# A fused transformer block on one core: three value products ahead of the loop's branch, spare weights kept in DRAM, rope products left in PSUM

## The reference, cut to what matters

```python
qkv = x @ w_qkv.T                       # 3 * 512 columns, 16 heads of 32
q, k = rope(q), rope(k)                 # pairs (even, odd) turned by cos and sin of the position
scores = q @ k.T * 32 ** -0.5           # only keys at most 63 rows back
attn = softmax(scores) @ v
x = layernorm(x + attn @ w_out.T)
gate = silu((x @ w_gate) * s_gate)      # int8 weights, 512 x 2048
up = (x @ w_up) * s_up
x = layernorm(x + ((gate * up) @ w_down) * s_down)
```

## Time and profile before

| | us |
|---|---|
| median of 3 runs | 1215.11 (1214.43 to 1217.15) |
| the profiled execution | 1210.73 |
| its span (first to last instruction) | 1208.9 |
| TensorE busy | 1159.1 (96%) |
| VectorE busy | 977.0 (81%) |
| ScalarE busy | 641.1 (53%) |
| GpSimd busy | 645.0 (53%) |
| mean granted TensorE clock, share of full | 0.991 |

### The profile page before, as it was taken

How to read it: one execution, slowest core, us unless ns; L and a number is a source line. 1 busy time by engine, 2 the same in 40 slices (tenths; PEclk the granted TensorE clock), 3 DMA queues, 4 the chain that set the end, 5 groups by cost and what they waited for, 6 DMA issues and landing times.

```text
span 1208.9 us, 25954 instructions
## 1 busy us (share of the span) xinstructions
PE 1159.1 (96%) x8601; PEld 606.4 (50%) x8601; DVE 977.0 (81%) x2727; ACT 641.1 (53%) x1777; POOL 645.0 (53%) x605
## 2 busy tenths in 40 slices
PE   9997999989999899998999989999899999999998
PEld 4444546445464454645446454464545546455444
DVE  7898988878887789877998779987699879986434
ACT  3954785038851479405794059922588127871330
POOL 0787675336753467525585166742577336752330
PEclk9999999999999999999999999999999999999999
DMA  9995895458844597534966269660795507944200
GB/s 289 181 183 120 152 201 127 105 85 158 138 105 109 81 171 136 130 76 72 193 116 148 57 94 197 115 144 36 124 180 110 136 36 142 194 85 105 87 1 35
DMA packets 360555, 149.78 MB, mean 124 GB/s; under 512 B 310096, under 2 KB 332752, under 8 KB 360400
## 3 DMA queue, kind: packets, MB, share of 16 engines
q1 hardware_dynamic: 334976, 106.86, 49.9%
q0 software_dynamic: 19008, 31.98, 9.3%
q10 hardware_dynamic: 6416, 9.00, 2.0%
HBM read 39.53 MB, written 8.39 MB: 40 GB/s over the span
## 4 chain that ended last, share of the span: by engine, by line
PE 55%; issue 16%; POOL 11%; DVE 8%; DMA 6%; ACT 3%; SPq 1%; POOLq 0%; DVEq 0%; ACTq 0%
PE bank L876 34%; PE bank L1148 18%; POOL fuse L768 7%; DMA y<-xT_sb 4%; POOL xT_sb L656 2%; PE bank L1083 2%; ACT bank L1384 1%; DVE fuse L1538 1%; POOL fuse L661 1%; DVE qkT L1601 1%; PE bank L1063 1%; DMA out<-x 1%; DMA xT_sb<-xT 1%; ACT fuse L1285 1%; PE bank L902 1%
## 5 line engine op out<-in xcount | busy, mean ns | idle before, releaser
L876 PE MATMUL bank<-x1T,wg 128*128 128x512 f16 (+1 forms) x1032 | 242.5, 378 | 1.2 <-DVE wg L1644 1.2
L876 PE MATMUL bank<-x1T,wu 128*128 128x512 f16 x1024 | 241.9, 379 | 0.0
L1384 ACT ACTIVATE bank<-bank,neg_max,qk_scale 128x128 f32<-128x128 f32 x512 | 220.3, 434 | 31.5 <-DVE neg_max L1693 30.3
L1148 PE MATMUL bank<-wd,fuse 128*128 128x512 f16 (+2 forms) x1056 | 222.7, 373 | 0.0
L661 POOL TENSOR_TENSOR fuse<-ffn_tmp,fuse 128x512 f16<-128x512 f32 x128 | 148.4, 1159 | 96.1 <-ACT fuse L1285 95.8
L768 POOL TENSOR_TENSOR fuse<-fuse 128x512 f16<-128x512 f32 x116 | 147.4, 1304 | 91.4 <-ACT fuse L1285 88.3
L656 POOL TENSOR_TENSOR xT_sb<-probs,xT_sb 128x512 f16<-128x512 f32 x112 | 129.9, 1160 | 79.4 <-ACT xT_sb L1285 79.2
L1148 PEld LDWEIGHTS bank<-wd,fuse 128*128 128x128 f16 x1056 | 101.9, 98 | 117.9
L876 PEld LDWEIGHTS bank<-x1T,wu 128*128 128x128 f16 x1024 | 100.2, 98 | 120.6
L876 PEld LDWEIGHTS bank<-x1T,wg 128*128 128x128 f16 x1032 | 96.4, 98 | 112.1 <-DVE wg L1644 1.4
L1295 ACT ACTIVATE ffn_tmp<-bank,tanh_scale 128x512 f32<-128x512 f32 x128 | 88.5, 692 | 72.1 <-PE bank L876 46.5
(11 more groups left out here) (238 smaller groups left out, 1903.4 us busy)
## 6 DMA issues: line engine op xcount, KB each, us to landing
wg<-w_gate POOLq DMA_DIRECT2D x16, 1024.0 KB, 5.3
wu<-w_up POOLq DMA_DIRECT2D x9, 1024.0 KB, 8.4
v_cross<-v_own SPq DMA_DIRECT2D x64, 128.0 KB, 3.1
out<-x ACTq DMA_DIRECT2D x31, 256.0 KB, 2.0
xT_sb<-xT SPq DMA_DIRECT2D x30, 256.0 KB, 3.8
qkT<-x SPq DMA_DIRECT2D x28, 256.0 KB, 3.4
wu<-w_up POOLq DMA_DIRECT2D x7, 512.0 KB, 5.8
wqkv<-w_qkvT SPq DMA_DIRECT2D x8, 256.0 KB, 6.5
```

The costliest lines, as they stand in the source:

```text
L876: last = pe.matmul(dst, lhsT, rhs, start=(i == 0 and not onto), stop=(i == len(pairs) - 1), skip_group_check=onto)
L1148: last = pe.matmul(dst[:, cols], fuse[:, s, z, rows], wd[:, s, cols], start=(s == 0 and z == 0), stop=(s == STEPS - 1 and z == 1))
L1384: last = act.activation(unit, unit, ACT.Exp, bias=neg_max[:, s % 2, h // 3, h % 3:h % 3 + 1], scale=qk_scale[:, 2:3], accum_out=row_sum[:, ...
```

## The change

- TensorE: `values_first(a, 0)`, `values_fifth(a, 0)` and `values_first(a, 1)` stand at the end of the pass before (`begin_values`), ahead of the branch. `values_first` waits for `rope_done` where it waited for `rope_read`.
- The three sums of the value weights are made once, in `first()`, stored to DRAM by GpSimd, and loaded each tile by ScalarE (768 KB) after the last `up`.
- The late columns are cast once to float16 in DRAM, in `first()`, and loaded from there by ScalarE behind `gate_tanh(f, 2)`, 1 MB and 768 KB (row 3 of `wu` is no longer overwritten); GpSimd's casting loads at step 2 are gone.
- ScalarE's order at the head of a pass: `split_high(2)` stands behind `keep_values_sixth(a, 1)`, and `keep_values_seventh(a, 1)` ahead of `split_high(3)`, where it stood behind `keep_v(a, 1)`.
- Rope: two of four products of a block are written back into their own bank, and the sums read one operand there.
- VectorE, end of attention: `keep_o(7)` and three `add_back_o` stand ahead of three of the four row sums of pair 0.

```diff
@@ gpsimd
+            def keep_v_weights():
+                pool.wait_ge(v_weights_added, 2)
+                pool.sem_inc(passed, 1)
+                pool.wait_ge(v_weights_in[0], 16)
+                pool.dma_start(kept_v_weights, wu[:, 0:KC - 1, LATE:].bitcast(F32)).then_inc(v_weights_kept, 16)
-            def reload_late_columns(a, f, attn):
-                wait(*((v_low, pool, a, NB - 1) if attn else (proj_read, pool, f, NB - 1)))
-                pool.sem_inc(passed, 1)
-                for src, dst in ((w_gate, wg), (w_up, wu)):
-                    done(late_columns_in, pool.dma_start(dst[:, :, LATE:],
-                                                         src.rearrange("(k p) n -> p k n", p=P)[:, :, LATE:]), 16)
...
+                pool.dma_start(wu[:, KC - 1:, LATE:], w_up.rearrange("(k p) n -> p k n", p=P)[:, KC - 1:, LATE:])\
+                    .then_inc(wffn_in, 16)
+                for src, kept, rows in ((w_gate, late_gate, slice(0, KC)), (w_up, late_up, slice(0, KC - 1))):
+                    pool.dma_start(kept, src.rearrange("(k p) n -> p k n", p=P)[:, rows, LATE:]).then_inc(late_kept, 16)
                 sum_w(3)
...
-                if more:
-                    add_v_weights(a + 1, f)
@@ tensor
             def values_first(a, i):
-                wait(rope_read, pe, a, i)
+                wait(rope_done, pe, a, i)
             def values_fifth(a, i):
                 wait(x_summed, pe, a - 1, 7)
-                wait(v_weights_added, pe, a - 1, 2)
+                wait(v_weights_in, pe, a - 1, 15)
-            def project_values(a):
+            def begin_values(a):
                 values_first(a, 0)
                 values_fifth(a, 0)
                 values_first(a, 1)
+
+            def project_values(a):
                 values_sixth(a, 0)
...
                 if more:
                     for i in range(2):
                         project_pair(a + 1, i)
+                    begin_values(a + 1)
@@ scalar
+            def reload_late_columns(a, f, attn):
+                wait(*((v_low, act, a, NB - 1) if attn else (proj_read, act, f, NB - 1)))
+                act.sem_inc(passed, 1)
+                act.wait_ge(v_weights_kept, 16)
+                act.sem_inc(passed, 1)
+                act.wait_ge(late_kept, 2 * 16)
+                for kept, dst in ((late_gate, wg[:, :, LATE:]), (late_up, wu[:, 0:KC - 1, LATE:])):
+                    done(late_columns_in, act.dma_start(dst, kept), 16)
+
+            def load_v_weights(f):
+                wait(up_done, act, f, STEPS - 1)
+                done(v_weights_in, act.dma_start(wu[:, 0:KC - 1, LATE:].bitcast(F32), kept_v_weights), 16)
...
                     keep_values_sixth(a, 0)
-                    split_high(a, 2, ffn)
                     keep_values_fifth(a, 1)
                     keep_values_seventh(a, 0)
                     keep_values_sixth(a, 1)
+                    split_high(a, 2, ffn)
+                    keep_values_seventh(a, 1)
                     split_high(a, 3, ffn)
                     keep_v(a, 0, ffn)
                     keep_v(a, 1, ffn)
-                    keep_values_seventh(a, 1)
...
                     gate_tanh(f, s)
+                    if s == 2:
+                        reload_late_columns(a, f, attn)
...
                 keep_fuse_high(f, STEPS - 1)
+                if more:
+                    load_v_weights(f)
@@ vector
-                    i = (0, 3, 1, 2)[part]
+                    i = ((3, 0, 1, 2) if ffn else (0, 3, 1, 2))[part]
                     src = (even, odd, odd, even)[i]
+                    dst = src if ffn and part % 2 else place[i]
...
-                dve.tensor_tensor(place[0], place[0], place[1], ALU.subtract)
-                done(rope_done, dve.tensor_tensor(place[2], place[2], place[3], ALU.add))
+                dve.tensor_tensor(place[0], even, place[1], ALU.subtract)
+                done(rope_done, dve.tensor_tensor(place[2], odd, place[3], ALU.add))
...
                     add_outer_kept(a, 0)
+                    keep_o(a, STEPS // 2 - 1)
+                    add_back_o(a, 1)
+                    add_back_o(a, 2)
+                    add_back_o(a, 3)
                     add_inner_kept(a, 0)
                     add_inner(a, 0)
                     add_outer(a, 0)
                     proj_added(a, 0)
-                    keep_o(a, STEPS // 2 - 1)
-                    add_back_o(a, 1)
-                    add_back_o(a, 2)
-                    add_back_o(a, 3)
```

More of the change, by code:

```diff
@@ L177, in build @@
         LAST_BANKS = (6, 7)
+        late_gate = nc.dram_tensor("late_gate", (P, KC, INTER // 2), F16, kind="Internal").ap()
+        late_up = nc.dram_tensor("late_up", (P, KC - 1, INTER // 2), F16, kind="Internal").ap()
+        kept_v_weights = nc.dram_tensor("kept_v_weights", (P, KC - 1, INTER // 4), F32, kind="Internal").ap()
         def ev(name, per_tile):
@@ L214, in build @@
         v_added = ev("v_added", NB)
-        v_weights_added = ev("v_weights_added", 3)
+        v_weights_added = sem("v_weights_added")
+        v_weights_kept = sem("v_weights_kept")
+        v_weights_in = ev("v_weights_in", 16)
         v_weights_lessened = sem("v_weights_lessened")
+        late_kept = sem("late_kept")
         o_product = ev("o_product", 12)
@@ L691, in lessen_v_weights, with add_v_weights @@
                 pool.tensor_tensor(low_right, low_right, low_left, ALU.subtract).then_inc(v_weights_lessened, 1)
-            def add_v_weights(a, f):
+            def add_v_weights():
                 low_left, right_less_left, high_left, high_right = v_quarters()
                 second, third, fourth = (added_v_weights(n) for n in range(3))
-                if isinstance(a, int) and a == 1:
-                    pool.wait_ge(v_weights_lessened, 1)
-                else:
-                    wait(up_done, pool, f, STEPS - 1)
-                done(v_weights_added, pool.tensor_tensor(second, high_right, right_less_left, ALU.subtract))
-                wait(v_weights_added, pool, a - 1, 0)
-                done(v_weights_added, pool.tensor_tensor(fourth, high_left, second, ALU.subtract))
-                done(v_weights_added, pool.tensor_tensor(third, second, low_left, ALU.subtract))
+                pool.wait_ge(v_weights_lessened, 1)
+                pool.tensor_tensor(second, high_right, right_less_left, ALU.subtract).then_inc(v_weights_added, 1)
+                pool.wait_ge(v_weights_added, 1)
+                pool.tensor_tensor(fourth, high_left, second, ALU.subtract).then_inc(v_weights_added, 1)
+                pool.tensor_tensor(third, second, low_left, ALU.subtract).then_inc(v_weights_in[0], 16)
+            def keep_v_weights():
[3 more added lines that the diff above has]
+                pool.dma_start(kept_v_weights, wu[:, 0:KC - 1, LATE:].bitcast(F32)).then_inc(v_weights_kept, 16)
             def sum_w(step):
@@ L812, in first @@
                 lessen_v_weights()
-                add_v_weights(a + 1, None)
+                add_v_weights()
+                keep_v_weights()
                 for j in range(2):
@@ L829, in body @@
                         split_fuse(f, s - 1)
-                    if s == 2:
-                        reload_late_columns(a, f, attn)
                     if attn and 5 <= s < 9:
@@ L1056, in scores @@
                 elif ffn:
-                    wait(rope_read, pe, a, 2 if s == 0 else NB - 1)
+                    wait(rope_done, pe, a, 2 if s == 0 else NB - 1)
                 for h in range(HG):
@@ L1237, in body @@
                     if s == 0:
-                        pe.wait_ge(wffn_in, 2 * 16)
+                        pe.wait_ge(wffn_in, 3 * 16)
                         for half in range(2):
@@ L1535, in rope_products @@
                 for part in parts:
-                    i = (0, 3, 1, 2)[part]
+                    i = ((3, 0, 1, 2) if ffn else (0, 3, 1, 2))[part]
                     src = (even, odd, odd, even)[i]
-                    last = dve.tensor_tensor(free_view(place[i], heads), free_view(src, heads), table(i), ALU.mult)
+                    dst = src if ffn and part % 2 else place[i]
+                    last = dve.tensor_tensor(free_view(dst, heads), free_view(src, heads), table(i), ALU.mult)
                 if parts[-1] == 3:
@@ L1543, in rope_sums @@
                 place = rope_place(j, ffn)
+                even, odd = qk_banks(j, ffn) if ffn else (place[0], place[2])
                 wait(rope_read, dve, a, j)
-                dve.tensor_tensor(place[0], place[0], place[1], ALU.subtract)
-                done(rope_done, dve.tensor_tensor(place[2], place[2], place[3], ALU.add))
+                dve.tensor_tensor(place[0], even, place[1], ALU.subtract)
+                done(rope_done, dve.tensor_tensor(place[2], odd, place[3], ALU.add))
             def first_split_low(j):
```

## The result

The changed kernel takes 1250.36 us (median of 4 runs, 1243.65 to 1254.41) against 1215.11 before: the ratio is 1.028, 95% interval 1.023 to 1.033. It is slower, as forecast, but by 35 us where 7 were predicted, and beyond the range's upper end of 1234. The profiled execution took 1247.43, its span is 1245.6, 36.7 longer than before; the mean granted clock is 0.974 (before 0.991).

What follows compares the result with a forecast made beforehand. TensorE, busy 96% of the span, was taken to bound the kernel, with the chain ahead of `gate(1)` and the reload cancelling the branch's gain: +12.6 - 2.6 = +10.0, hence 1222 on the median, range 1201 to 1234.

Steps and rivals of the forecast that it cites:

- The branch: At the back edges: 32 queued instructions fit and cover most of TensorE's 5.0 branch, leaving a gap of about 1.
- P4: Fourth value product, forecast to start 5.6 behind `pair_fourth` instead of 9.55; bounds 4.4 and 9.6.
- rope at 0: Rope sums: shortening them from 1.7 to 0.7 gains 0, as that chain waits for products anyway.
- The chain ahead of `gate(1)`: ScalarE and VectorE copies after P4: `gate(1)` comes 17.3 behind P4, with TensorE idle 3.3 and then at reduced clock.
- Rival (a): Faster: the chain does not bind, `add_v(3)` comes by P4 + 14; -23, giving 1199; chance 0.18.
- The reload: Late-column loads ahead of step 1's transpose: `weigh_v(1)` 14.4 behind `gate(1)` instead of 11.5; bounds 12.6 and 16.2.
- The gain at `weigh_v(2)` and `(3)`: Waits for turned probabilities, 1.62 a tile, go because step 2 is turned behind the reload.
- the value-weight load: 2 us of DMA beside step 15's transpose, with 1.9 of slack: 0, bound +0.5 a tile.
- 0, or +2: GpSimd's added work in `first()`, four DMA issues and a store: 4 us with cover, costing 0 or +2.
- The 0.41 in the output projection: Wait ahead of the third product of pair 1 all but goes: 7 x 0.37 = -2.6.
- The sum: All terms together: +12.6 - 2.6 = +10.0, taking the profiled execution from 1210.73 to 1220.7.
- (d): Slower: the reload takes as long as before, +1.8 x 7, giving 1234; chance 0.10.

Runs made afterwards that it cites:

- c1: Kernel before with only the three value products moved ahead of the loop's branch; 1207.71 us, ratio 0.995.
- f1: c2 plus the change's VectorE order at the end of attention, GpSimd's cast reload cut into four parts at its steps 2 to 5; 1183.64 us, ratio 0.971.
- h1: f1 with the rope products of the change, partly left in PSUM; 1178.16 us, ratio 0.969.
- g1: Changed kernel with the three value products behind the branch again and ScalarE's copies in the old order; 1251.56 us, ratio 1.030.
- a3: Changed kernel with ScalarE copying keep_v(0) and (1) ahead of keep_values_seventh(1) and split_high(3); 1241.83 us, ratio 1.022.
- g2: b1 without the two casting stores to DRAM in first(); 1187.06 us, ratio 0.977.
- a4: Changed kernel with ScalarE loading the value weight sums behind the last copy of the output products; 1252.5 us, ratio 1.030.
- a2: Changed kernel with ScalarE issuing the DRAM reload at step 3, once the transpose of step 1 has landed; 1225.78 us, ratio 1.009.
- c2: c1 plus the ScalarE copy order of a3, on the kernel before; 1192.96 us, ratio 0.983.
- b1: Changed kernel with GpSimd's cast reload at step 2 again, the copy order of a3 and the late value-weight load of a4; 1193.74 us, ratio 0.982.

## Why the prediction was right in sign and wrong in size

**The branch: right.** That 32 instructions fit into TensorE's queue, so that the branch lies under them, is what happened; P4 came at 4.5 to 4.7, nearer to the lower bound of 4.4 than to the 5.6 taken. The branch itself stayed, about 0.4 shorter than the 4.8 to 5.0 of the earlier trace rows:

```profile
L488 PEldq COMPARE_BRANCH  x6: 83/4432/4527, 267.0 to 1032.5; - x6
```

It starts at 421.46, 0.4 ahead of `pair_fourth`, where before it started 0.1 behind it; the earlier start and the shorter branch together make the 0.9. c1, f1 and h1 show where this comes from: without the rope products in PSUM the branch starts 0.4 behind `pair_fourth` and leaves 0.5 to 0.7 of "issue"; with them, none. Putting rope at 0 was an error of about 0.5 for each edge here, and more in `first()`; at edges where the products stay behind the branch (g1) up to 9.6 in all. The prediction had the reason in hand ("1.7 against 0.7") and took it for a chain that nothing waits for.

**The chain ahead of `gate(1)`: right.** P4 to `gate(1)` was predicted as 17.3 and is 17.4; the gap of 3.3 is 3.2, in all seven tiles, with the releaser that was named; tile 1, whose P4 comes at 8.5 before and after, lost 3.3 by it where 2.6 were taken. a3 shows that its cause is the one given, `split_high(3)` ahead of `keep_v`. Only the clock was too dark: it stayed at 1.00 behind two of the seven. Rival (a) is out; with the order of a3 nothing waits ahead of `gate(1)`, but that is not this change.

**The reload: the mechanism right, the term mis-sized.** The step that failed is "1792 KB at the 387 GB/s of the plain loads of 15 to 20 take 4.7; ... step 1's transpose lands 0.9 to 1.1 later", hence 14.4. `weigh_v(1)` came 16.8 behind `gate(1)` in the mean (14.1 to 20.3), above even the bound of 16.2: 4.9 a tile more than before, not 2.9. The moment of issue was right for this tile (7.0 behind `gate(1)`; 7.1 measured) and for tile 6; in the others, by the half clock, it was 7.5 to 9.0, which the prediction did not see, and which made their transposes earlier against it, not later. The rate was not right: the two loads took 9.1 from the first issue to the last landing in this tile, and 9.2 to 15.5 in the others, not 6.3. (The sum for 6.3 also has a slip: 440.1 + 1.3 + 4.7 is 446.1, not 446.4. The 1.3 ahead of the first byte stands in no row; the first packets of the reload came 1.3 to 2.4 behind its issue.) The 387 GB/s were read from a stretch with nothing else in the queues, while here the two `v_cross` copies and two transposes of SyncE run beside them: the DMA view of 451 to 464 has 2698 packets of SyncE's queue (q1) against 928 of ScalarE's (q10), at 228 GB/s in all:

```profile
DMA packets 3628, 2.97 MB, mean 228 GB/s; under 512 B 2474, under 2 KB 2474, under 8 KB 3626
...
q10 hardware_dynamic: 928, 1.84, 45.7%
q1 hardware_dynamic: 2698, 1.11, 44.1%
```

Before, GpSimd's two loads took 8.1 to 10.4 from the first issue (443.29) to the last landing, with 256 KB more; the earlier trace rows were the rows to take, with the 0.8 between the two issues added. They give 9.3 for the reload, and with 1.1 for the transpose behind it 17.3; even my upper bound, 16.2, had it take only 8.2. As the Trainium skill puts it ("DMA: Bandwidth & Descriptors", "Queues, rings and completion order": engines take their queues in turn), ScalarE's queue held up SyncE's as GpSimd's did; 8.9 against 3.0 agree.

**The gain at `weigh_v(2)` and `(3)`: the second step that failed.** "In exchange the 1.62 ... go" counted -11.3. The waits did go, but not the time: where the wait at `weigh_v(1)` was over 5 (tiles 2, 3, 5 and 6) the granted clock was 0.50 to 0.57 behind it, and `weigh_v(2)` came 9.3 to 10.3 behind `weigh_v(1)`; in tiles 1, 4 and 7 it came 7.7 behind, as predicted. A longer gap costs once as a gap and again in the clock; I had priced the second half of it behind `gate(1)` only. The rest of this row of the table is the value-weight load (six waits, 4.8 in all), which was put at 0 with 1.9 of slack and a bound of +0.5 a tile. It measured up to 0.9, for the transpose of step 15 was issued 0.3 behind it:

```profile
518.74 0.29 PE L1089 MATMUL bank<-y,v_cross 128*32 128x128 f16 x8 [0.93 <-DMA y<-xT_sb]
```

**`first()` and the sums.** "0, or +2" was +2.5. It had been looked for as lateness of GpSimd's own work, not as VectorE being held up beside it: the two row operations take 7.24 instead of 3.66. g2 shows that without the stores most of this is gone; a3, with the stores and 1.06, shows that they are not the whole cause. The 0.41 in the output projection went in all tiles, as predicted.

**The sum.** +10.0 predicted and +36.7 measured. The nearest rival was (d), the reload as slow as before: right in kind, but with its price counted only up to 16.2 and with the clock left out it ended at 1234.

Some things stay open. Why the reload takes 14 to 16 in five cases was not tried: the transpose falls 0.2 to 0.3 behind its issue in four of them (tile 5, three tiles of a4), but 0.9 in tile 5 of a3, and in the last tile of a4 the reload takes 10.0 with 0.2. Nor is it shown that 1.0 ahead is enough, though the last tile took 3.0: a4 has 7.3 and 7.5 at 1.0 in tiles 3 and 5, and the last tile takes 3.0 to 3.1 in every kernel whose transpose goes first, while tiles 1 to 6 take 3.5 to 5.0 even where no reload has been issued yet (a2). A kernel in which ScalarE's parts are issued without blocking its queue was not built.

## What to carry to other kernels

Price a bulk transfer at its new place by the rows of that place, with everything that shares the DMA engines, and ask which small transfer on the critical path is issued just behind it: here some 3 us in the moment of issue decided 30 us in 1250, and moving three products, worth 1.7% with a fitting order of copies (c2), was buried in this change until both the transfer's place and that order were put right (b1). A wait long enough to drop TensorE's clock is paid twice, so a sum over gaps alone is a lower bound; and a changed clock also moves what other engines issue, so the order of two transfers can differ from tile to tile. When work is moved forward, look at every in-order engine that serves it, since its old order (c1) can take back most of the gain.

## What the runs showed of the hardware

- ScalarE's sequencer issues a DMA far ahead of its engine's work in program order: the reload written behind `gate_tanh(2)` went out at 451.05, when the engine was in the exponentials of step 2, ahead of that `gate_tanh` (451.86). It still goes in order: the waits of that `gate_tanh` have to be met first, and so it went out 7.1 to 9.0 behind `gate(1)`.
- The DMA transpose of step 1 took 3.1 to 4.8 with a load of 1.8 or 2 MB issued 1.3 to 3.2 behind it (3.0 to 5.0 where the load was only issued after it had landed), 7.1 to 7.7 with 0.9 to 1.0 (3.0 once, in the last tile), and 8.5 to 12.8 when it was the one behind. So 1.3 was enough here, and 1.0 in most cases was not.
- A taken branch of 4.3 to 4.7 on TensorE's sequencer left no gap behind 32 queued instructions where it started 0.4 ahead of their first one (the changed kernel, h1), and one of 0.5 to 0.7 where it started 0.4 behind (c1, f1).
- 1.8 MB of plain copies and 2 MB of cast loads took the same 8 to 11 beside the transposes (14 to 16 in five tiles of the plain copies); the smaller volume bought nothing.
- Two VectorE row operations (128x512, float32) took 3.7 to 4.5 beside two or three DMA issues of GpSimd and the operations behind them, and 6.9 to 7.7 beside five, but 1.06 beside five in a3.
- Two rope sums that read two SBUF operands took 1.7 and 1.6 in one block of each pass of the kernel before; with one operand in PSUM they take 0.7 in every block.
